# Pairwise embedding tower: other loads and another order of work in the first stage

## The reference

```
e = jnp.stack([tbl_0[ids[:, 0]], ..., tbl_31[ids[:, 31]]], axis=1)
p = e[:, ROW]; q = e[:, COL]                   # ROW, COL: the 496 pairs of fields
kp = jnp.einsum('bpj,ipj->bpi', p, kernel)
z = jnp.sum(kp * q, axis=-1)
h = jnp.concatenate([z, dense_ctx], axis=1)
h = jnp.maximum(h @ W_top1 + b_top1, 0.0)
h = jnp.maximum(h @ W_top2 + b_top2, 0.0)
y = h @ W_top3
```

## Time and profile before

| | us |
|---|---|
| median of 3 runs (lowest, highest) | 451.44 (450.06, 451.81) |
| profiled execution | 451.3 |
| its span, first to last instruction | 449.5 |
| PE busy | 428.2 (95%) |
| VectorE busy | 302.9 (67%) |
| POOL busy | 230.5 (51%) |
| ScalarE busy | 70.5 (16%) |

### The profile page before, as it was taken

How to read it: one execution, slowest core, us unless ns; L and a number is a source line. 1 busy time by engine, 2 the same in 40 slices (tenths; PEclk the granted TensorE clock), 3 DMA queues, 4 the chain that set the end, 5 groups by cost and what they waited for, 6 DMA issues and landing times.

```text
span 449.5 us, 10096 instructions
## 1 busy us (share of the span) xinstructions
PE 428.2 (95%) x4290; PEld 283.0 (63%) x4290; DVE 302.9 (67%) x324; ACT 70.5 (16%) x154; POOL 230.5 (51%) x248
## 2 busy tenths in 40 slices
PE   0769999999999999999999999999999999999997
PEld 0447666767676766767676676767676766664442
DVE  4466687786878686886788787877887787860000
ACT  1002211102021111011221110111211201101122
POOL 4775776556576656565767574747674300000000
PEclk9989999999999999999999999999999999999999
DMA  5663444342111111110111110111151000000000
GB/s 141 199 192 80 126 123 125 100 131 62 22 40 39 25 33 25 20 41 18 39 36 30 29 28 19 39 23 37 31 177 33 14 1 14 1 1 1 0 0 0
DMA packets 15316, 23.55 MB, mean 52 GB/s; under 512 B 5505, under 2 KB 7809, under 8 KB 15144
## 3 DMA queue, kind: packets, MB, share of 16 engines
q1 hardware_dynamic: 6884, 14.14, 10.4%
q0 software_dynamic: 7808, 8.01, 9.3%
q10 hardware_dynamic: 580, 0.76, 0.6%
HBM read 20.79 MB, written 0.00 MB: 46 GB/s over the span
## 4 chain that ended last, share of the span: by engine, by line
PE 95%; DMA 3%; issue 1%; ACT 0%; SPq 0%
PE kp L535 52%; PE z_ps L552 25%; PE kp L573 6%; PE tr_ps L519 5%; PE tr_ps L511 3%; PE kp L579 3%; DMA k_sb<-in_tbl 3%; PE kp L586 0%; ACT pair L393 0%; ACT prod L437 0%; SPq L332 0%; SPq L338 0%; SPq L341 0%
## 5 line engine op out<-in xcount | busy, mean ns | idle before, releaser
L481 DVE TENSOR_TENSOR prod<-kp,pair 128x1024 f32<-128x1024 f32 x224 | 259.0, 1216 | 83.9 <-PE kp L535 83.9
L375 POOL DMA_INDIRECT raw<-in_tbl,ids_sb x244 | 230.3, 944 | 122.1 <-issue 67.0
L535 PE MATMUL kp<-pair,k_sb 64*128 64x256 f32 x1984 | 238.8, 387 | 0.0
L535 PEld LDWEIGHTS kp<-pair,k_sb 64*128 64x128 f32 x1984 | 182.9, 187 | 41.9 <-DVE prod L481 11.3
L552 PE MATMUL z_ps<-prod,ones_sel 128*32 128x256 f32 x1984 | 117.0, 382 | 0.0
L552 PEld LDWEIGHTS z_ps<-prod,ones_sel 128*32 128x32 f32 x1984 | 59.7, 110 | 50.5 <-issue 10.7
L393 ACT ACTIVATE pair<-tr_ps 128x256 f32<-128x256 f32 x64 | 24.5, 383 | 247.4 <-PE tr_ps L519 218.6
L511 PE MATMUL tr_ps<-prod,k_sb 125*64 125x256 f32 x96 | 14.3, 464 | 17.9 <-DMA k_sb<-in_tbl 13.4
L491 DVE TENSOR_TENSOR prod<-kp,pair 128x512 f32<-128x512 f32 x48 | 30.0, 681 | 0.0
L573 PE MATMUL kp<-z_sb,k_sb 128*128 128x512 f32 x64 | 28.0, 596 | 0.0
L519 PEld LDWEIGHTS tr_ps<-ident,raw 128*128 128x128 f32 x122 | 12.3, 141 | 24.2 <-issue 23.3
(11 more groups left out here) (9 smaller groups left out, 7.4 us busy)
## 6 DMA issues: line engine op xcount, KB each, us to landing
k_sb<-in_kd SPq DMA_DIRECT2D x15, 512.0 KB, 4.1
raw<-in_tbl,ids_sb POOLq DMA_INDIRECT x244
pair<-pair SPq DMA_DIRECT2D x32, 64.0 KB, 2.3
k_sb<-in_tbl SPq DMA_DIRECT2D x6, 250.0 KB
k_sb<-in_w SPq DMA_DIRECT2D x1, 1024.0 KB
hot_ids_sb<-in_hot_ids SPq DMA_DIRECT2D x3, 250.0 KB
z_sb<-in_dense ACTq DMA_DIRECT2D x1, 512.0 KB, 8.8
k_sb<-in_w SPq DMA_DIRECT2D x1, 512.0 KB
```

The lines of the kernel that those rows point to most:

```text
L375: nc.gpsimd.indirect_dma_start(raw[:, r % RAW_RING, i, n, :], None, tables[f], bass.IndirectOffsetOnAxis(ap=ids_sb[:, 2 * b + i, f:f + 1], ...
L481: nc.vector.tensor_tensor(prod[:, u % PROD_RING, :, :].rearrange("p q (i n) -> p (q i) n", i=UNIT_SLOTS), kp[u % KP_RING][:, :, :].rearran ...
L535: last = nc.tensor.matmul(kp[u % KP_RING][:, q, i * WIDTH:(i + 1) * WIDTH], k_sb[rows, x, :], pair[rows, group_place(st, owner // 2), :], ...
```

## The change

- The three pairs of tables of the looked-up groups come as one array `small`, padded with zeros from 1000 to 1024 rows, so that ids and tables span 128 partitions; one load a group in place of two. VectorE compares both fields of a group in one instruction of 512 columns.
- SP's first loads are now ids, tables, ids, tables, ids, tables, then the first half piece of pair kernels. SP then waits for all three tables before it issues the next pieces.
- `row_no` is loaded by ScalarE's queue, ahead of the ids. The ids come in two pieces, the first stage's first; the dense values are loaded by SP behind unit 24.
- POOL writes zeros to a corner of `z_sb`, and PE begins with nine products of these zeros (`WARM`).
- Event 1 goes to `z_ps` in place of `tr_ps`, so that PE doesn't wait for the evacuation of event 0 there. `consts_in` is awaited at the first transpose only.
- In `TRANSPOSE_AT` three events of the first stage move: from unit 9 to 10, 15 to 16 and 25 to 28.

The groups that are looked up are the same in both kernels.

```diff
-SMALL = 1000
-SMALL_P, SMALL_C = 125, 8
+SMALL, SMALL_C = 1000, 8
+WARM = 9
+DENSE_AT = 24
-TRANSPOSE_AT = [0, 0, 0, 1, 2, 3, 7, 9, 13, 15, 20, 23, 25, 31, 36, ...
+TRANSPOSE_AT = [0, 0, 0, 1, 2, 3, 7, 10, 13, 16, 20, 23, 28, 31, 36, ...
-        K_LOADS = [(j, min(j + K_LOAD, SLOTS)) for j in range(0, SLOTS, K_LOAD)]
+        K_LOADS = [(0, K_LOAD // 2), (K_LOAD // 2, K_LOAD)]
+        K_LOADS += [(j, min(j + K_LOAD, SLOTS)) for j in range(K_LOAD, SLOTS, K_LOAD)]
+        K_LOAD_AT = {first: j for j, (first, end) in enumerate(K_LOADS)}
+        def event_ps(e):
+            return z_ps if e == 1 else tr_ps
             def load_hot_ids(i):
-                sp.dma_start(hot_ids_sb[0:SMALL_P, i, :, :],
-                             hot_ids[i:i + 1, :, :].broadcast_to([SMALL_P, 2, WIDTH])).then_inc(hot_ids_in[i], 16)
+                sp.dma_start(hot_ids_sb[:, i, :],
+                             hot_ids[i:i + 1, :].broadcast_to([P, 2 * WIDTH])).then_inc(hot_ids_in[i], 16)
             def load_tables(i):
-                for n in range(2):
-                    table = tables[2 * LOOKUP[i] + n].rearrange("(p c) e -> p c e", c=SMALL_C)
-                    sp.dma_start(table_sb[0:SMALL_P, i, n, :, :], table).then_inc(table_in[i], 16)
-
-            load_hot_ids(0)
-            sp.dma_start(row_sb[0:SMALL_P, :], row_no).then_inc(row_no_in, 16)
-            load_tables(0)
-            load_hot_ids(1)
-            load_tables(1)
+                sp.dma_start(table_sb[:, i, :, :, :], small[:, i, :, :, :]).then_inc(table_in[i], 16)
+
+            for i in range(len(LOOKUP)):
+                load_hot_ids(i)
+                load_tables(i)
             load_k(0)
-            load_hot_ids(2)
-            load_tables(2)
+
+            for i in range(len(LOOKUP)):
+                sp.wait_ge(table_in[i], 16)
             for j in range(1, K_AHEAD):
                 load_k(j)
...
-                j = s // K_LOAD
-                if st == 0 and s % K_LOAD == 0 and j + K_AHEAD < len(K_LOADS):
+                if u == DENSE_AT:
                     sp.wait_ge(kp_done, u + 1)
-                    load_k(j + K_AHEAD)
+                    sp.dma_start(z_sb[:, FC - 1, :], dense).then_inc(dense_in, 16)
+                if st == 0 and s in K_LOAD_AT and K_LOAD_AT[s] + K_AHEAD < len(K_LOADS):
+                    sp.wait_ge(kp_done, u + 1)
+                    load_k(K_LOAD_AT[s] + K_AHEAD)
...
+            nc.gpsimd.memset(z_sb[:, 0, 0:WIDTH], 0.0).then_inc(zeros_ready, 1)
             pool.wait_ge(ids_in, 16)
...
-            act.dma_start(ids_sb[:, :, :], ids).then_inc(ids_in, 16)
+            act.dma_start(row_sb[:, :], row_no).then_inc(row_no_in, 16)
+            act.dma_start(ids_sb[:, 0:WIDTH // P, :], ids[:, 0:WIDTH // P, :]).then_inc(ids_in, 16)
             act.dma_start(ident[:, :], ident_in).then_inc(consts_in, 16)
             act.dma_start(ones_sel[:, :], sel_in).then_inc(consts_in, 16)
-            act.dma_start(z_sb[:, FC - 1, :], dense).then_inc(dense_in, 16)
+            act.dma_start(ids_sb[:, WIDTH // P:, :], ids[:, WIDTH // P:, :]).then_inc(ids_rest_in, 16)
...
                 for c in range(SMALL_C):
-                    for n in range(2):
-                        nc.vector.tensor_scalar(hot(i, n, c), hot_ids_sb[0:SMALL_P, i, n, :],
-                                                row_sb[0:SMALL_P, c:c + 1], None,
-                                                ALU.is_equal).then_inc(hot_ready, 1)
+                    nc.vector.tensor_scalar(hot(i, c), hot_ids_sb[:, i, :], row_sb[:, c:c + 1], None,
+                                            ALU.is_equal).then_inc(hot_ready, 1)
...
-            pe.wait_ge(consts_in, 2 * 16)
+            pe.wait_ge(zeros_ready, 1)
+            for i in range(WARM):
+                nc.tensor.matmul(kp[KP_RING - 1][:, 1, 0:WIDTH], z_sb[:, 0, 0:P], z_sb[:, 0, 0:WIDTH],
+                                 start=True, stop=True)
...
-                if e:
-                    pe.wait_ge(evacuated, e)
+                if e > 1:
+                    pe.wait_ge(evacuated, e if e > 2 else 1)
...
-                    pe.wait_ge(table_in[lookup], 2 * 16)
+                    pe.wait_ge(table_in[lookup], 16)
                     for c in range(SMALL_C):
+                        pe.wait_ge(hot_ready, SMALL_C * lookup + c + 1)
                         for i in range(2):
-                            pe.wait_ge(hot_ready, 2 * (SMALL_C * lookup + c) + i + 1)
-                            last = nc.tensor.matmul(tr_ps[64 * i:64 * i + 64, 0:WIDTH],
-                                                    table_sb[0:SMALL_P, lookup, i, c, :], hot(lookup, i, c),
+                            last = nc.tensor.matmul(event_ps(e)[64 * i:64 * i + 64, 0:WIDTH], table_sb[:, lookup, i, c, :],
+                                                    hot(lookup, c)[:, i * WIDTH:(i + 1) * WIDTH],
                                                     start=(c == 0), stop=(c == SMALL_C - 1), skip_group_check=True)
                 for r in raws:
+                    if r == 0:
+                        pe.wait_ge(consts_in, 2 * 16)
```

More of the change, by code:

```diff
@@ L229, in dense_row, with pairwise_tower @@
     return 32 * (n // (32 - used)) + used + n % (32 - used)
-def pairwise_tower(nc, dense, ids, hot_ids, row_no, tables, kd, ident_in, sel_in, w1, b1, w2, b2, w3, out):
+def pairwise_tower(nc, dense, ids, hot_ids, row_no, small, tables, kd, ident_in, sel_in, w1, b1, w2, b2, w3, out):
     from contextlib import ExitStack
@@ L248, in pairwise_tower @@
         w3_sb = sb("w3_sb", [P, N2, 32])
-        hot_ids_sb = sb("hot_ids_sb", [P, len(LOOKUP), 2, WIDTH], I32)
+        hot_ids_sb = sb("hot_ids_sb", [P, len(LOOKUP), 2 * WIDTH], I32)
         row_sb = sb("row_sb", [P, SMALL_C])
@@ L260, in pairwise_tower, with hot @@
             "p (i n c e) -> p i n c e", i=len(LOOKUP), n=2, c=SMALL_C)
-        def hot(i, n, c):
-            at = (SMALL_C * n + c) * WIDTH
-            return prod[0:SMALL_P, HOT_UNITS * i + at // (2 * ROWS), at // ROWS % 2, at % ROWS:at % ROWS + WIDTH]
+        def hot(i, c):
+            return prod[:, HOT_UNITS * i + c // 2, c % 2, :]
         W_SLOTS = (FC * HID1 + N1 * HID2) // P
@@ L367, in _ @@
         def _(pool):
+            nc.gpsimd.memset(z_sb[:, 0, 0:WIDTH], 0.0).then_inc(zeros_ready, 1)
             pool.wait_ge(ids_in, 16)
             for r, (g, b) in enumerate(GATHER):
+                if b and not GATHER[r - 1][1]:
+                    pool.wait_ge(ids_rest_in, 16)
                 if r >= RAW_RING and EVENT_OF[r - RAW_RING] != (EVENT_OF[r - RAW_RING - 1] if r > RAW_RING else None):
@@ L393, in evacuate @@
                 nc.scalar.activation(pair[:, group_place(st, k):group_place(st, k) + n, :],
-                                     tr_ps[:, 0:n * WIDTH].rearrange("p (n w) -> p n w", n=n),
+                                     event_ps(e)[:, 0:n * WIDTH].rearrange("p (n w) -> p n w", n=n),
                                      ACT.Copy).then_inc(evacuated, 1)
@@ L518, in transpose_event @@
                         to = (g - k) * WIDTH + i * P
-                        last = nc.tensor.transpose(tr_ps[:, to:to + P],
+                        last = nc.tensor.transpose(event_ps(e)[:, to:to + P],
                                                    raw[:, r % RAW_RING, i, :, :].rearrange("p a n -> p (a n)"),
@@ L528, in products @@
                 for i, x in enumerate(unit_slots(u)):
-                    if st == 0 and x % K_LOAD == 0:
-                        pe.wait_ge(k_in[x // K_LOAD], 16)
+                    if st == 0 and x in K_LOAD_AT:
+                        pe.wait_ge(k_in[K_LOAD_AT[x]], 16)
                     for q in range(2):
@@ L616 @@
     tables = [tables[f] for f in field_at]
+    small = _np.zeros((2 * len(LOOKUP), P * SMALL_C, EMBED), _np.float32)
+    for i in range(len(LOOKUP)):
+        for n in range(2):
+            small[2 * i + n, 0:SMALL] = tables[2 * LOOKUP[i] + n]
+    small = small.reshape(len(LOOKUP), 2, P, SMALL_C, EMBED).transpose(2, 0, 1, 3, 4)
     pair_no = {}
@@ L649 @@
     ids = ids_in.reshape(BLOCKS, P, FIELDS).transpose(1, 0, 2)
-    hot_ids = _np.stack([ids_in[0:WIDTH, 2 * k:2 * k + 2].transpose(1, 0) for k in LOOKUP])
-    row_no = _np.arange(SMALL, dtype=_np.float32).reshape(SMALL_P, SMALL_C)
+    hot_ids = _np.stack([ids_in[0:WIDTH, 2 * k:2 * k + 2].transpose(1, 0).reshape(-1) for k in LOOKUP])
+    row_no = _np.arange(P * SMALL_C, dtype=_np.float32).reshape(P, SMALL_C)
     sel = _np.zeros((P, 64), _np.float32)
@@ L654 @@
     sel[64:128, 31] = 1.0
-    arrays = {"dense": dense_rows, "ids": ids, "hot_ids": hot_ids, "row_no": row_no, "ident": _np.eye(P, dtype=_np.float32), "sel": sel}
+    arrays = {"dense": dense_rows, "ids": ids, "hot_ids": hot_ids, "row_no": row_no, "small": small, "ident": _np.eye(P, dtype=_np.float32), "sel": sel}
     for f in range(FIELDS):
@@ L666 @@
     out = nc.dram_tensor("out_y", (HALVES, ROWS), _mybir.dt.float32, kind="ExternalOutput").ap()
```

(2 more changed lines are left out.)

4 lines of the change are left out of this document (3 added, 1 removed).

## The result

The changed kernel took 447.22 us, median of 6 runs (443.18 to 448.95), beside 451.5 us (450.06 to 452.85) for the kernel before: a ratio of 0.990 [0.985, 0.995]. So it is faster, by 4.3 us in the medians and not by 14, and it lies outside the range of 435.2 to 440.3. The profiled execution took 448.95 us with a span of 447.1; before it was 451.3 and 449.5. The six spans run from 441.3 to 447.1 us, a wider spread than before, and the profiled execution is the slowest of the six: what its trace shows is not what each of them did.

The account below looks back on a forecast made before the run. Early on, the landing of POOL's gathers was to bound PE, which runs without a gap afterwards. The transpose ahead of unit 13 comes 14.0 us earlier: 451.3-14.0 = 437.3, so 437.4 us for the median; range 435.2 to 440.3.

Parts of the forecast that it names:

- The sign: Whole kernel: the change makes it faster, by more than half a per cent, with chance 0.96.
- the sum: First-stage transposes: gathers' landings set how much earlier each can be; the smallest gain, 14.0 us, counts.
- r = 5: Gathered group transposed ahead of unit 13: start moves from 49.41 to 35.4 us, 14.0 earlier, the smallest gain listed.
- the 1.2 us of room of PE's chain: PE's work up to event 5 allows at most 15.2 us earlier, against 14.0 by the gathers.
- the pace is POOL's own: POOL's gathers: 1.25 us each whatever the traffic, 4.99 us a group, unchanged by the change.
- The ids' landing: Start: first ids, second in ScalarE's queue, let the first gather begin at 3.9 us, bounds 3.6 and 4.93.
- The bound of 4.93: Start: latest begin assumed for the first gather, the same as in the kernel before.
- The landing of r = 0: Any group: time from its last gather's end until landed, taken as 1.7 us, bounds 0.9 and 2.8.
- Zeros: PE's start: nine products of zeros end near 6.8 us, bounds 5.2 and 9.1.
- The compares: VectorE's 512-column compares: 0.58 us each, ends 0.53 and 0.63; groups ready at 8.9, 13.6 and 18.2.
- rival 1: PE's own chain ends later than the gathers: 438.4 us with slow zeros, 440.1 if the clock also falls; chance 0.16.
- Rival 4: Held-back pair kernels come too late: 459.8 us in full (unit 2), chance 0.03; mild (unit 8) 438.6, chance 0.05.

Follow-up runs that it names:

- the best version: Changed kernel with first ids as SP's first load and compares of 256 columns over 125 partitions, an increment each, no pauses: 438.93 us, 0.972.

## Why the prediction was wrong

The sign held, and so did the structure in the main: behind the first groups PE does bound the kernel without a gap, tables over 128 partitions came in time, and the landing of gathers did set where PE stands. But the sum took the wrong group for it. It lists r = 2, 3, 5, 6 and 8 and lets r = 5 decide. In the changed kernel and in the best version the group that decides is r = 0, which the list leaves out; behind its transpose PE waited for no gather. By the prediction's own figures r = 0 landed at 10.44 and PE could take it at 6.8+3.67 = 10.47. So only the 1.2 us of room of PE's chain lay between it and the 14.0, and each microsecond beyond that went straight into the time.

**The step that failed** is "the pace is POOL's own, 1.25 us a gather, in crowded and quiet stretches alike, and stays". The earlier trace rows showed gathers beside compares, but only such as had begun first: 4.93 against 6.49. In the changed kernel the ids came behind the row numbers and the compares were one stream. In the profiled execution, the slowest, the first gather cost 7.79 us, 6.7 more than its like, and the idle time of PE that followed another 2.3 us of clock in the second lookup. That the compares hold the gather is shown by its end: in all seven traces with a hold of over 3 us the gather ended 0.12 to 0.96 us behind the stream, be the stream 9.6 or 12.7 us long and the DMA engines full or idle. That it hangs on when each starts is shown from both sides: late ids put the hold into a kernel that hadn't it, a late stream took it out of two that had. It is no rule without exception, as the gathers of 1.21 and 1.14 us show. The spreads, such as 442 to 453 us with 256 columns, fit executions in which the gather came through and others in which it was held; that is inferred, since none of the quick ones was profiled. What lets one gather into a running stream and not another stays open.

**The ids' landing** was mis-sized: 3.9 to the first gather became 7.51. I took the identity load's 2.6 us from a start in which loads ran on 5 engines. With 16, the small load waited behind the very loads that the change speeds up (6.05 us; 1.78 as SP's first). The first gather began 3.6 us later for it, which made the hold possible. By itself, with nothing held, it cost some 2.5 us (441.43 with late ids, 438.93 with early ones). The bound of 4.93 ("as now") was no bound.

**The landing of r = 0**, 1.7, was right in the quiet (in the changed kernel the last gather ended at 19.05, the transpose began at 20.67). Beside table loads it was 5.3 in the best version, outside the bounds of 0.9 to 2.8. The upper bound was taken from the 18th gather of the kernel before and not from a start with all tables under way.

**Terms that held or didn't matter.** Zeros ended at 7.46, 6.8 forecast within 5.2 to 9.1. The compares took 0.400 each, not 0.53 to 0.63: I had carried a pace that was slowed by gathers beside it (0.31 for 256; alone 0.264) and saved too little for the fixed part (256 more columns cost 0.136). The clock fell as in rival 1, but behind a wait of 9.6 us, not of one, for 2.3 us and not 1.7. Rival 4 did not come about in the changed kernel: no wait for pair kernels showed.

With the ids early and nothing held the time comes back to 438.9 us against 437.4, inside the range, with the unit-13 transpose at 36.99 against 35.4. It gets there by another path, so the nearness is in part luck: PE takes r = 0 at 12.97 and not at 10.5, 2.5 us late, and never waits for r = 5, for which the forecast had about 1.2 us.

## What to carry to other kernels

Before you speed up the loads that feed VectorE, list what GpSimd issues in that stretch, and which of the two starts first: a pace read off rows in which the gathers were first says nothing of the other order. Load first the few kilobytes on which the long chain (ids, gather, transpose) waits; engines that are filled well make small loads behind them late. If VectorE has slack, one wait can make it start with the gathers and not ahead of them. When you list the times at which things land, begin with the first one that is waited for. And look at several executions: where the spread is wide, one trace shows one case of several.

## What the runs showed of the chip

- A stream of tensor_scalar compares (0.264 us for 256 columns, 0.400 for 512, so the 256 more cost 0.136, or 1.9 columns a ns) held a gather that arrived in it until the stream ended: 7.79, 8.97, 11.78, 11.79 and 11.80 us in five profiled executions. In two others (512 columns, over 125 partitions, and over 128 with pauses) the gather that arrived came through in 1.21 and 1.14 us; in the former the fourth was held for 3.26. An increment behind each compare didn't let it in. As tensor_tensor (0.62 us for 512) the stream held none in the one profiled execution.
- With gathers running first or starting with the stream, compares of 256 columns gave way (0.31) and gathers kept 0.94; compares of 512 kept 0.400, and gathers took up to 1.28, or one was held (7.61). Why the width decides that is open.
- A held gather ended 0.95 or 0.96 us behind a stream of 256 columns, about as long as a gather takes alone, but 0.12 or 0.13 us behind one of 512.
- A 32 KB load took 1.7 to 1.9 us as the first in line and some 6 behind wide loads; PE could take a gathered group 1.6 us behind its last gather in a quiet stretch and some 5 in a crowded one.
